# Chebyshev mixing of a graph network: scores and weighted half batches move to a PSUM bank, dense products share three banks

## The reference, cut to what matters

```python
n = x.shape[0]
feats = [_cheb(x, prop, w2, b2), _cheb(x, prop, w3, b3), _cheb(x, prop, w4, b4)]
concat = jnp.concatenate(feats, axis=1)
scale_w = jax.nn.softmax(concat @ attn_w + attn_b, axis=1)
fused = jnp.concatenate([feats[i] * scale_w[:, i:i + 1] for i in range(3)], axis=1)
h = fused @ fus_w + fus_b
mean = jnp.mean(h, axis=0)
var = jnp.mean((h - mean) ** 2, axis=0)
h = (h - mean) * jax.lax.rsqrt(var + BN_EPS) * bn_gamma + bn_beta
```

## Time and profile before

| | us |
|---|---|
| median of 3 runs | 14526.22 (14521.36 to 14529.68) |
| the profiled execution, its own time | 14521.27 |
| its span in the profile | 14519.6 |
| PE busy | 5141.8 (35%) |
| DVE busy | 8613.3 (59%) |
| ACT busy | 3939.6 (27%) |
| POOL busy | 8127.0 (56%) |
| gathers of cheb1, L527, x392 | 447.0, mean 1140 ns |
| dense products L1594, MATMUL x1568 | 561.8, mean 514 ns |

### The profile page before, as it was taken

The page is one execution under the profiler, slowest core; times in us unless marked ns, Lnnn a source line. Parts: engine busy times, 40 slices in busy tenths (PEclk is TensorE's granted clock), DMA queues, the critical chain, the costliest instruction groups (busy, mean ns, idle before and its releaser), DMA issues. The chain is left out here.

```text
span 14519.6 us, 105608 instructions
## 1 busy us (share of the span) xinstructions
PE 5141.8 (35%) x25061; PEld 4156.3 (29%) x25061; DVE 8613.3 (59%) x14550; ACT 3939.6 (27%) x10228; POOL 8127.0 (56%) x8280
## 2 busy tenths in 40 slices
PE   0000002000000001200005444576767977888876
PEld 0000002000000001100005334455546976666554
DVE  8870345444444445522477678776755778568865
ACT  0000011000000001100262342266644257654431
POOL 0557777777777777777407750177763000640767
PEclk9955555555555555555555555587878965899555
DMA  6200234433433444411375433344466667777753
GB/s 218 112 5 1 52 90 138 118 114 113 118 114 113 118 114 122 129 54 54 125 239 161 129 118 108 108 140 131 137 208 225 229 239 272 244 252 242 224 168 110
DMA packets 955385, 2071.04 MB, mean 143 GB/s; under 512 B 318121, under 2 KB 323519, under 8 KB 938640
## 3 DMA queue, kind: packets, MB, share of 16 engines
q1 hardware_dynamic: 689040, 1702.87, 34.3%
q0 software_dynamic: 265728, 361.43, 11.1%
HBM read 1251.36 MB, written 822.13 MB: 143 GB/s over the span
## 5 line engine op out<-in xcount | busy, mean ns | idle before, releaser
L731 POOL DMA_INDIRECT hop_raw<-hop_table,i_hop x2352 | 2219.5, 944 | 734.3 <-issue 686.3
L527 POOL DMA_INDIRECT gine_raw<-x,i_near x392 | 376.2, 960 | 1433.4 <-POOLq L89 1314.2
L755 DVE TENSOR_TENSOR hop_rows<-hop_raw,hop_factors 128x672 f32<-128x672 f32 x336 | 289.8, 863 | 1494.4 <-DMA hop_raw<-hop_table,i_hop 1494.4
L825 PE MATMUL hop_rows<-hop_chain,src_carries 128*128 128x96 f32 x12 | 4.3, 450 | 3023.6 <-DVE hop_chain L801 3023.6
L833 ACT ACTIVATE hop_keeps<-src_inner 128x672 f32<-128x672 f32 x336 | 255.4, 762 | 2664.9 <-DVE hop_chain L801 2613.0
L527 POOL DMA_INDIRECT cheb_raw<-cheb_table,i_cheb x784 | 817.0, 1042 | 245.1 <-issue 236.5
L825 PEld LDWEIGHTS hop_rows<-hop_chain,src_carries 128*128 128x128 f32 x12 | 3.0, 311 | 3024.9 <-issue 3024.9
L527 POOL DMA_INDIRECT cheb_raw<-x,i_near x392 | 447.0, 1140 | 647.8 <-POOLq L89 528.6
L527 POOL DMA_INDIRECT gine_raw<-conv,i_near x392 | 395.7, 1009 | 603.4 <-POOLq L89 484.2
L1803 POOL DMA_INDIRECT own_raw<-x,i_dst x392 | 388.2, 990 | 594.7 <-POOLq L89 475.6
L1594 PE MATMUL cheb_base_product<-folded,cheb_base_turned_rows 97*128 97x292 f32 x1568 | 561.8, 514 | 180.0 <-ACT cheb_base_mixed L1553 180.0
(11 more groups left out here) (538 smaller groups left out, 21337.1 us busy)
## 6 DMA issues: line engine op xcount, KB each, us to landing
hop_res<-hop_table SPq DMA_DIRECT2D x336, 336.0 KB
hop_table<-hop_sums SPq DMA_DIRECT2D x336, 336.0 KB
part<-cheb_put_mixed SPq DMA_DIRECT2D x49, 1168.0 KB
cheb_slots_ends_part<-part SPq DMA_DIRECT2D x49, 1168.0 KB
start_x_x<-x_and_map SPq DMA_DIRECT2D x98, 400.0 KB, 3.7
x<-start_x_rows SPq DMA_DIRECT2D x98, 400.0 KB
cheb_base_term<-x SPq DMA_DIRECT2D x98, 400.0 KB
mid<-cheb_base_rows SPq DMA_DIRECT2D x98, 400.0 KB, 4.5
```

Source lines behind the costliest of these rows:

```text
L527: pool.indirect_dma_start(out=raw_rows[:, b % RAW, g, :], out_offset=None, in_=table, in_offset=bass.IndirectOffsetOnAxis(ap=index[:, t:t ...
L731: pool.indirect_dma_start(out=raw_rows[:, b % RAW, g, :], out_offset=None, in_=table, in_offset=bass.IndirectOffsetOnAxis(ap=index[:, t:t ...
L755: nc.vector.tensor_tensor(by_channel(b).rearrange("p c t -> p t c"), raw[:, b % RAW, :, :], spread(weights[:, at], C), ALU.mult).then_inc( ...
L825: nc.tensor.matmul(carried, side.carries[:, :], chain[:, (batches - 1) % LINES, :, EDGE - 1], start=True, stop=True).then_inc(s["carried"], 1)
```

## The change

The scores and one weighted half batch now lie in one PSUM bank, `weigh`: columns 0 to 383 are the weighted half batch, 384 to 431 the scores of two batches. This holds for the dense form and for cheb_slots. The weighting becomes one full-width product into `rows`, and then for each half batch and each of the other two blocks a product into PSUM and a sum from it, with a wait behind each.

The bank is taken from the dense products: they take turns in three banks, `(4 * q + c) % 3`, and TensorE waits for the evacuation of the product three before instead of four before (`place_free`). The forms "put" and "ends" keep four banks, and their waits are what they were. Two SBUF tiles go (6,144 and 192 bytes a partition).

```diff
-            self.score, self.most, self.mask = (self.sb(ph, "score", [P, 2, self.GROUP, 3]),
-                                                self.sb(ph, "most", [P, self.GROUP]), self.sb(ph, "mask", [P, 2, self.GROUP]))
-            self.part = self.sb(ph, "weighted", [P, 2, self.GROUP, C])
+            self.most, self.mask = self.sb(ph, "most", [P, self.GROUP]), self.sb(ph, "mask", [P, 2, self.GROUP])
+            weigh = ph.psum(f"{self.tag}_weigh", [P, 512])
+            self.weighted = weigh[:, 0:4 * C].rearrange("p (g c) -> p g c", c=C)
+            self.score = weigh[:, 4 * C:4 * C + 6 * self.GROUP].rearrange("p (n g s) -> p n g s", n=2, s=3)
             self.sum = ph.psum(f"{self.tag}_sum", [C, 512])
...
-        self.product = [ph.psum(f"{self.tag}_product{n}", [P, 512]) for n in range(4)]
+        self.places = 4 if self.part_out or self.narrow else 3
+        self.product = [ph.psum(f"{self.tag}_product{n}", [P, 512]) for n in range(self.places)]
...
-    def taken_one(self, ph, eng, q, c):
-        if self.part_out:
-            eng.wait_ge(self.sem(ph, "moved" if c % 2 else "taken"), 2 * q + c // 2 + 1)
-        else:
-            eng.wait_ge(self.sem(ph, "taken"), 4 * q + c + 1)
+    def place_free(self, ph, eng, q, c):
+        before = 4 * q + c - self.places
+        if before >= 0 and self.part_out:
+            eng.wait_ge(self.sem(ph, "moved" if c % 2 else "taken"), before // 2 + 1)
+        elif before >= 0:
+            eng.wait_ge(self.sem(ph, "taken"), before + 1)
...
-            def weighted(n):
-                return self.mixed[:, m, :, n * C:(n + 1) * C], spread(score[:, :, n], C)
-            own.step(nc.vector.tensor_tensor(rows, *weighted(0), ALU.mult))
-            own.step(nc.vector.tensor_tensor(self.part[:, 0, :, :], *weighted(1), ALU.mult))
-            own.step(nc.vector.tensor_tensor(self.part[:, 1, :, :], *weighted(2), ALU.mult))
-            own.wait()
-            own.step(nc.vector.tensor_tensor(rows, rows, self.part[:, 0, :, :], ALU.add))
-            own.wait()
-            own.step(nc.vector.tensor_tensor(rows, rows, self.part[:, 1, :, :], ALU.add))
-            own.wait()
+            def weighed(into, g, n):
+                own.step(nc.vector.tensor_tensor(into, self.mixed[:, m, g, n * C:(n + 1) * C], spread(score[:, g, n], C),
+                                                 ALU.mult))
+            weighed(rows, slice(0, self.GROUP), 0)
+            for g in (slice(0, 4), slice(4, 8)):
+                for n in (1, 2):
+                    weighed(self.weighted, g, n)
+                    own.wait()
+                    own.step(nc.vector.tensor_tensor(rows[:, g, :], rows[:, g, :], self.weighted, ALU.add))
+                    own.wait()
             dve.sem_inc(self.sem(ph, "ready"), 1)
...
-            if q:
-                self.taken_one(ph, pe, q - 1, c)
-            into = self.product[c][:, 0:MIX]
+            self.place_free(ph, pe, q, c)
+            into = self.product[(4 * q + c) % self.places][:, 0:MIX]
```

More of the change, by code:

```diff
@@ L1456, in vector @@
                 dve.wait_ge(self.sem(ph, "product"), 4 * q + c + 1)
-                self.nc.vector.tensor_tensor(into, into, self.product[c][:, 0:MIX], ALU.add)\
+                self.nc.vector.tensor_tensor(into, into, self.product[(4 * q + c) % self.places][:, 0:MIX], ALU.add)\
                     .then_inc(self.sem(ph, "taken"), 1)
@@ L1552, in scalar @@
                 act.wait_ge(self.sem(ph, "product"), 4 * q + c + 1)
-                nc.scalar.activation(self.mixed[:, m, q % 2 * 4 + c, :], self.product[c][:, 0:MIX], ACT.Copy)\
+                what = self.product[(4 * q + c) % self.places][:, 0:MIX]
+                nc.scalar.activation(self.mixed[:, m, q % 2 * 4 + c, :], what, ACT.Copy)\
                   .then_inc(self.sem(ph, "taken"), 1)
```

## The result

The changed kernel takes 14666.33 us (median of four runs, 14664.87 to 14666.91) against 14525.52 for the kernel before on the same chip (four runs, 14521.36 to 14529.68): a ratio of 1.0096 [1.008, 1.0112], 141 us slower. The forecast was 14690, 24 us more, and the range held the time. The profiled execution of the change took 14666.7 us, 145.4 more than that of before (14521.3); the two executions are compared from here on.

What follows compares the result with a forecast made beforehand. Bound: a loop of waits in the edge passes, TensorE in cheb_slots. Two passes 133 us plus cheb_slots 34 make 167 on the profiled 14521.3 us: 14688, say 14690; range 14620 to 14780.

Steps and rivals of the forecast that it cites:

- What bounds the kernel: Edge passes cheb1 and cheb2: a loop of waits, no engine busy throughout; cheb_slots: TensorE, busy 604.6 of 620 us.
- Mix-first batches: Edge batches where VectorE weights before the scores; weighting and ScalarE's evacuations run in series, 12.6 us a batch before.
- scores-first: Edge batches where VectorE does the scores before the weighting and is the bound, 9.48 us a batch before.
- The weighting, 0.88 for the steps and 0.9 with the scores: VectorE, each weighting: 5.57 us instead of 4.69, and 0.02 more for each of two score steps writing PSUM.
- Product 3: Dense product waiting for the bank of product 0 under three banks: 0.9 us more per mix-first batch, hidden in scores-first ones.
- the low bound: Whole kernel: weighting 0.65 us longer, product 3 at TensorE's upper clock costing 0.2, cheb_slots 0.45 a batch: 14617 us.
- The two passes: cheb1 and cheb2: longer weighting in every batch plus late product 3 in mix-first ones, 67 us each, 133 together.
- cheb_slots, 34 us: Stage cheb_slots: TensorE stalls 0.7 us a batch behind the longer weighting (0.9 less 0.2 slack), 49 times.
- GpSimd, nothing: Gathers go back to about 0.94 us, but nobody waits for them, so the saving becomes GpSimd waiting for free buffers.
- Dearer PSUM steps: Rival: VectorE's PSUM half steps cost more than 0.55 us, 0.51 more a weighting, 75 us, giving 14765; chance 0.15.
- Gathers as the bound: Rival: GpSimd's gathers bound the edge passes, so 78 us a pass comes back and the kernel takes 14399; chance 0.04.
- Cover unseen: Rival: the longer weighting falls into a wait that shortens as much, total within 29 us of before; chance 0.06.

Runs made afterwards that it cites:

- e3: Kernel before, with the change's one full-width product and eight half-width steps, but weighted half batch and scores in SBUF, four banks: 14657.84 us, 1.0092.
- e2: Kernel before, with the new weighting and its PSUM bank in cheb_slots alone, dense form unchanged with four banks: 14565.30 us, 1.0026.
- e4: Kernel before, with scores in the PSUM bank and three product banks, but the weighting in five full-width steps in SBUF: 14545.88 us, 1.0011.
- e5: Kernel before, with the dense form's mixing steps dealt out two to an edge batch from the first on: 14462.78 us, 0.9949.
- e1: Kernel before, with the dense products in three banks, scores and weighting as they were: 14551.55 us, 1.0015.

## Why the prediction was right, point by point

*What bounds the kernel.* Right. Mix-first batches stayed a loop through weighting and evacuations, scores-first ones a busy VectorE, cheb_slots a busy TensorE; each grew by what its path got.

*The weighting, 0.88 for the steps and 0.9 with the scores.* Start to end it takes 5.57 us, as forecast from 0.55 and 0.57 a half step: the measured 553 and 561 ns with their gaps make the same sum. The splitting costs it, not PSUM: e3 has 558 ns for the sums from SBUF. The small part for the scores had the wrong sign: the two steps that write PSUM did get 0.01 us longer each, but the exponent, which was put at nothing, and the mask step got shorter by more, 1.82 to 1.69 us in all. So a scores-first batch grew by 0.77 instead of 0.9.

*Product 3, "0.9 us more in a mix-first batch".* **This is the term that was mis-sized.** The mechanism is there: between 9400 and 9990 ScalarE waited 95 times for TensorE at an evacuation, and in the mix-first ones this wait is on the path. But it typically moves the fourth evacuation by 1.26 - 0.92 = 0.34 us, and 0.88 + 0.34 = 1.22 is the 1.21 that the batch grew by. Of the late product the passes were the part that was read wrongly: 0.76 us, where the prediction took 1.34 from the product that stood there in the old order. That row was no odd one: in cheb1 before, the passes took 1.34 us in 16 of 23 mix-first batches, and 0.76 to 1.16 in the other seven, which the prediction did not look at. In the new order the lower level came there twice in 23, and then the batch did take 14.3 to 14.4 us. Why TensorE was at its upper level so much more often there is not shown by any run. The prediction had worked out 0.2 for that level, with half of 1.34 us for the passes, and kept it for the low bound; 0.34 came.

The two passes were forecast at 133 us and took 97. Of the 36 between, 29 lie in the mix-first batches and those with one step, 5 in the scores-first ones, and 2 come from counting 49 batches a pass where there are 48 intervals.

*cheb_slots, 34 us.* Right: 35.4 in the change, 34.8 alone in e2, with TensorE's stall of 0.70 us a batch where 0.7 was worked out.

*GpSimd, nothing.* Right. The gathers went to 944 ns and GpSimd waited 92.8 us for ScalarE instead. The reason given for it, fewer steps with two SBUF inputs, is borne out by e4, where gathers stretch beside such steps alone. It is not the only way: e3 keeps such steps, in halves, and has 977.

*What was not in the sum.* Some 13 us lie outside the stretches between weightings, among them 5.8 before the first weighting of cheb1 (9401.16 to 9406.97), 4.9 before that of cheb2 and 4.5 behind the last one of cheb_slots. The kernel of three banks shows such a rest also, some 5 of its 24 us. Part of it need not come from the change: e2, whose code up to cheb_slots is that of the kernel before, also starts its first weighting 4.5 us later, and takes 10.0 us more behind its last one in cheb_slots. Between the passes e2 lost nothing, so the 4.9 there may be the change's own; which wait makes it was not tried. That this rest made up for a third of the terms that were too large, and brought the forecast within 24 us, is luck.

*The rivals.* Dearer PSUM steps: fallen, by 561 and 553 ns against the 0.61 it needed. The table on which the Trainium skill, "VectorE: DVE Perf Modes", in the section on the TRN2 errata, puts a source in PSUM at more than one in SBUF is not borne out by these steps: 384 columns take 553 ns from PSUM and 558 from SBUF. Gathers as the bound: fallen for this order, since they got 0.2 us shorter and every batch longer; e5 shows the pace at which it comes true. Cover unseen: fallen, every batch grew.

## What to carry to other kernels

Count what a split of VectorE steps adds in fixed parts before crediting it with anything: four more instructions and the lost overlap cost 0.88 us a weighting here, and the engine that it relieved had nobody waiting for it. Read the price of a step that moves from every place in the trace that is like its new one, not from a single row, and where these differ, as TensorE's levels did in 7 of 23, give the term both values. When batches of the same work come in two lengths, look at what sets their order before changing the steps: here a two-line edit to the sharing out of steps gave 69 us, and with the scores in PSUM 137.

## What the runs showed of the hardware

- TensorE's level cannot be told from the idle time ahead alone: products after 2.65 us (the change) and 3.31 us (e1) of idle took 0.76 us for two passes, products after 2.60 and 2.87 us (the change) and 3.51 took 1.34.
- A gather on GpSimd takes 0.94 us alone, and took 1.37 (e4), 1.45 (e3) and 1.68 beside full-width VectorE steps with both inputs in SBUF. Beside a full-width step with one input in PSUM it took 0.94 (e4). Beside half-width steps with both inputs in SBUF and waits between them it took 0.94, and VectorE's step 0.62 instead of 0.56 (e3). The Trainium skill, "SBUF — State Buffer", in the section on who interferes with whom, speaks of an exclusive lock on the port that the two share; these runs agree that one of the two pays, and show that it is GpSimd beside the long steps with two SBUF inputs and at times VectorE in short ones.
- An exponent of 128x24 on ScalarE took 175 ns with source and target in PSUM, and 0.22 us in SBUF.
